# Quantised activations held as float16 multiples of 2^-24 instead of integers with an offset

## The reference

```python
u = (mu @ W_dec + b_dec).reshape(B, 257, 30)      # mu = cond: 2 x 128
param = einsum('bik,kj->bij', u, V)               # rank 30, V: 30 x 256
y = x @ param[:, :-1] + param[:, -1]              # x: 2 x 1024 x 256
quant_act(a)    = round(a * 127/max|a|_row) / (127/max|a|_row)
quant_weight(w) = clip(round(w / s), -1, 1) * s   # s = mean|w|
h = gelu(quant_act(y) @ quant_weight(w1).T)       # w1: 1024 x 256
out = x + quant_act(h) @ quant_weight(w2).T       # w2: 256 x 1024
```

## Time and profile before

| | us |
|---|---|
| median of 3 runs | 70.28 |
| lowest, highest | 69.92, 72.28 |
| profiled execution, its time | 69.81 |
| profiled execution, its span from the first to the last instruction | 68.0 |
| PE busy | 57.9 |
| DVE busy | 45.2 |
| ACT busy | 36.1 |
| POOL busy | 28.7 |

### The profile page before, as it was taken

One profiled execution on the slowest core, in us unless ns is written; L12 is line 12 of the kernel. 1 busy time (PEld: TensorE's weight loads), 2 busy tenths in 40 slices (PEclk: granted clock), 3 DMA queues, 4 the chain that ended last, 5 costly groups with the idle time before them and its releaser, 6 DMA issues.

```text
span 68.0 us, 1313 instructions
## 1 busy us (share of the span) xinstructions
PE 57.9 (85%) x463; PEld 31.8 (47%) x469; DVE 45.2 (66%) x92; ACT 36.1 (53%) x53; POOL 28.7 (42%) x46
## 2 busy tenths in 40 slices
PE   2977599998796799979999969999999999979910
PEld 0324132222432364433564823855859577869800
DVE  2000708475428784899999898499796979996520
ACT  3506005700067297999987826747959293753000
POOL 6500000000000109996848894674675828970000
PEclk9999999999999999999999999999999999999999
DMA  0899999999999999400199969699698999923052
GB/s 0 183 379 422 409 414 415 419 383 396 412 412 424 438 400 448 198 19 0 26 195 46 225 126 193 123 183 194 126 258 36 230 260 212 360 89 154 22 200 96
DMA packets 18343, 16.20 MB, mean 238 GB/s; under 512 B 14752, under 2 KB 15136, under 8 KB 17952
## 3 DMA queue, kind: packets, MB, share of 16 engines
q1 hardware_dynamic: 18192, 15.86, 77.8%
q10 hardware_dynamic: 144, 0.24, 2.0%
HBM read 10.47 MB, written 2.10 MB: 185 GB/s over the span
## 4 chain that ended last, share of the span: by engine, by line
PE 38%; DMA 20%; DVE 15%; SPq 9%; ACT 8%; issue 4%; POOL 2%; DVEq 0%
DMA w_dec_all<-in_w_dec_dram 17%; PE ps_h L471 13%; PE ps_o L492 8%; PE ps_z L492 6%; SPq L254 5%; ACT w_dec_all L617 4%; DMA yq_t<-yq_h 4%; DVE pair_max L726 3%; DVE h_max L744 3%; PE ps_y L443 3%; DVE o_sb L768 3%; SPq L271 2%; PE ps_z L431 2%; POOL hq_h L371 2%; ACT y_q L606 1%
## 5 line engine op out<-in xcount | busy, mean ns | idle before, releaser
L371 POOL TENSOR_SCALAR hq_h<-w_dec_all,pair_rcp 128x1024 f16<-128x1024 f32 x14 | 15.7, 1118 | 7.9 <-DVE pair_rcp L740 7.2
L471 PE MATMUL ps_h<-w_t,yq_t 128*128 128x512 bf16 x60 | 15.1, 380 | 1.4 <-DMA yq_t<-yq_h 0.7
L726 DVE TENSOR_REDUCE pair_max<-w_dec_all 128x2 f32<-128x2048 f32 x7 | 15.9, 2277 | 0.0
L617 ACT ACTIVATE w_dec_all<-ps_h,pair_c 128x1024 f32<-128x1024 f32 x10 | 10.9, 1113 | 6.6 <-PE ps_h L471 6.6
L397 PE MATMUL ps_h<-warm_h 128*128 128x512 bf16 x37 | 11.5, 424 | 1.5 <-POOL warm_h L313 1.3
L471 PEld LDWEIGHTS ps_h<-w_t,yq_t 128*128 128x128 bf16 x64 | 5.6, 98 | 8.4 <-issue 1.3
L329 POOL TENSOR_TENSOR c<-y_inv,s 128x2 f32<-128x2 f32 x3 | 0.6, 193 | 20.5 <-DVE y_inv L714 20.5
L492 PE MATMUL ps_o<-w_t,hq_t 128*128 128x256 f16 x64 | 8.3, 273 | 0.4 <-DVE o_sb L768 0.4
L492 PE MATMUL ps_z<-w_t,hq_t 128*128 128x256 f16 x64 | 8.3, 273 | 0.0
L589 ACT ACTIVATE w_abs<-w_sb 128x1024 f32<-128x1024 f32 (+1 forms) x3 | 2.7, 914 | 9.4 <-DMA w_sb<-in_w_tr_dram 9.3
L617 ACT ACTIVATE w_dec_all<-ps_h,c 128x1024 f32<-128x1024 f32 x6 | 6.8, 1133 | 0.5 <-PE ps_h L471 0.5
(11 more groups left out here) (90 smaller groups left out, 70.9 us busy)
## 6 DMA issues: line engine op xcount, KB each, us to landing
w_sb<-in_w_tr_dram SPq DMA_DIRECT2D x4, 512.0 KB, 9.0
x_sb<-in_x_dram SPq DMA_DIRECT2D x2, 1024.0 KB, 18.8
out_dram<-o_sb SPq DMA_DIRECT2D x7, 256.0 KB, 2.7
w_dec_all<-in_w_dec_dram SPq DMA_DIRECT2D x3, 512.0 KB, 7.9
w_dec_all<-in_w_dec_dram SPq DMA_DIRECT2D x3, 448.0 KB, 8.5
x_t<-in_x_tr_dram SPq DMA_DIRECT2D x1, 1024.0 KB, 16.5
w_dec_all<-in_w_dec_dram SPq DMA_DIRECT2D x1, 576.0 KB, 10.6
x_t<-in_x_tr_dram SPq DMA_DIRECT2D x2, 256.0 KB, 11.1
```

The lines of the kernel that those rows point to most:

```text
L371: pool.tensor_scalar(hq_h[n % NB][:, :], h_tile(n), scale, H_OFFSET, ALU.mult, ALU.add).then_inc(hq_ready, 1)
L471: last = nc.tensor.matmul(ps_h[k][:, half, :], yq_t[:, p, n % 2, c, :], w1_t[:, c, half * HALF:(half + 1) * HALF], start=(c == 0), stop=(c ...
L617: nc.scalar.activation(h_tile(n), ps_h[n % 2][:, :, :].rearrange("p a n -> p (a n)"), ACT.Gelu, scale=c1_of(n)).then_inc(gelu_done, 1)
L726: nc.vector.tensor_reduce(pair_max[:, p, 2:4], h_pair[p % NH], AXX, ALU.max, apply_absolute_value=True).then_inc(pair_max_ready, 1)
```

## The change

Rows are scaled by 127 * 2^-24 / max instead of 127 / max. The results are at most 127 multiples of 2^-24, the spacing of the smallest float16 numbers, so that a write to float16 rounds them to whole multiples with no offset. y_q becomes float16 and is transposed as it is, by PE or by the DMA; the copies out of PSUM move bit patterns as int16 and subtract nothing; w1's ternary values become float16. `narrow_y`, `offset_sums`, the copy on ACT, and the matmul with `offsets` in `product_2` go. The waits follow: SP's transpose_yq waits for ACT's quantise_y, and quantise_y(6) and (7) wait until the DMA has read the buffer of pairs 4 and 5. The 2^-24 is taken back by the factors per row, which are computed from the same scaled maxima. The diff, cut to its core:

```diff
-OFFSET = 16384.0
-MAGIC = 1.5 * 2 ** 23 + OFFSET
-H_OFFSET = 1024.0 + 128.0
+UNIT = 2.0 ** -24
...
-ident_h = sb("ident_h", [P, P], BF16)
-offsets = sb("offsets", [P, P], FP16)
-w1_t = sb("w1_t", [P, DC, H], BF16)
+w1_t = sb("w1_t", [P, DC, H], FP16)
-w2_off = sb("w2_off", [P, D], FP16)
...
-y_q = [sb(f"y_q{k}", [P, 2, D]) for k in range(2)]
-yq_h = [sb(f"yq_h{k}", [P, 2, D], BF16) for k in range(2)]
-yq_t = sb("yq_t", [P, NP, 2, DC, P], BF16)
+y_q = [sb(f"y_q{k}", [P, 2, D], FP16) for k in range(2)]
+yq_t = sb("yq_t", [P, NP, 2, DC, P], FP16)
...
-def low_half(t):
-    return t.bitcast(BF16).rearrange("p (n two) -> p n two", two=2)[:, :, 0]
-def blocks(bank, n, dt=BF16):
-    return bank[:, 0:n * P // 2].bitcast(dt).rearrange("p (c q) -> p c q", c=n)
-yq_low = [low_half(y_q[k][:, :, :].rearrange("p t c -> p (t c)")) for k in range(2)]
+def blocks(bank, n):
+    return bank[:, 0:n * P // 2].bitcast(FP16).rearrange("p (c q) -> p c q", c=n)
+yq_flat = [y_q[k][:, :, :].rearrange("p t c -> p (t c)") for k in range(2)]
-ps_off = ps_o[:, 0:D]
...
     def transpose_yq(p):
-        sp.wait_ge(yqh_ready, p - 3)
-        sp.dma_start_transpose(yq_t[:, p, :, :, :].rearrange("p t c q -> p (t c) q"),
-                               yq_h[p % 2][:, :, :].rearrange("p t c -> p (t c)")).then_inc(yqt_landed[p % 2], 16)
+        sp.wait_ge(yq_ready, 2 * p + 2)
+        sp.dma_start_transpose(yq_t[:, p, :, :, :].rearrange("p t c q -> p (t c) q"), yq_flat[p % 2]).then_inc(yqt_landed[p % 2], 16)
     def transpose_hq(n):
...
-    def narrow_y(p):
-        pool.wait_ge(yq_ready, 2 * p + 2)
-        if p >= 6:
-            pool.wait_ge(yqt_landed[p % 2], yqt_count(p - 2))
-        pool.tensor_scalar(yq_h[p % 2][:, :, :].rearrange("p t c -> p (t c)"),
-                           y_q[p % 2][:, :, :].rearrange("p t c -> p (t c)"), 1.0, -MAGIC,
-                           ALU.mult, ALU.add).then_inc(yqh_ready, 1)
     def part_of(w, n):
...
-        pool.tensor_scalar(hq_h[n % NB][:, :], h_tile(n), scale, H_OFFSET, ALU.mult, ALU.add).then_inc(hq_ready, 1)
+        pool.tensor_scalar(hq_h[n % NB][:, :], h_tile(n), scale, None, ALU.mult).then_inc(hq_ready, 1)
...
-        if 1 <= p < LATE_Y - AHEAD:
-            narrow_y(p + AHEAD)
-    pool.tensor_scalar(hq_h[(NT - 1) % NB][:, HALF:], h_tile(NT - 1)[:, HALF:], h_rcp[:, NT - 1:NT], H_OFFSET,
-                       ALU.mult, ALU.add).then_inc(last_hq[1], 1)
+    pool.tensor_scalar(hq_h[(NT - 1) % NB][:, HALF:], h_tile(NT - 1)[:, HALF:], h_rcp[:, NT - 1:NT], None,
+                       ALU.mult).then_inc(last_hq[1], 1)
...
     def total(k, part):
-    def offset_sums():
-        pe.wait_ge(yqt_copied, EARLY_YQT)
-        for n in range(2):
-            pe.wait_ge(s_w2q[n], 1)
-        pe.wait_ge(s_identf, 1)
-        for t in range(HC):
-            last = nc.tensor.matmul(ps_off, ident_f[:, :], w2_t[:, t, :], start=(t == 0), stop=(t == HC - 1))
-        last.then_inc(s_offsum, 1)
     def product_z(q, halves=range(DC)):
...
-            last = nc.tensor.transpose(ps_yqt[n][:, c - DC * i0, :], yq_low[p % 2][:, c * P:(c + 1) * P], ident_h[:, :])
+            last = nc.tensor.transpose(ps_yqt[n][:, c - DC * i0, :], yq_flat[p % 2][:, c * P:(c + 1) * P], ident_f[:, :])
     def product_1(n):
...
     def product_2(n):
-            pe.wait_ge(s_offs, 1)
-            pe.wait_ge(s_w2off, 1)
+            pe.wait_ge(yqt_copied, EARLY_YQT)
+            for part in range(2):
+                pe.wait_ge(s_w2q[part], 1)
-            nc.tensor.matmul(o_of[n], offsets[:, :], w2_off[:, :], start=True, stop=False)
-            last = nc.tensor.matmul(o_of[n], hq_t[k][:, t, :], w2_t[:, t, :], start=(n >= LATE and t == 0), stop=(t == HC - 1))
+            last = nc.tensor.matmul(o_of[n], hq_t[k][:, t, :], w2_t[:, t, :], start=(t == 0), stop=(t == HC - 1))
     def transpose_hq(n, half):
...
     def quantise_y(p):
-            act.wait_ge(yqh_ready, p - 5)
+            act.wait_ge(yqt_landed[p % 2], yqt_count(p - 2))
...
-                                 bias=MAGIC, scale=scale).then_inc(yq_ready, 1)
+                                 scale=scale).then_inc(yq_ready, 1)
     def gelu(n):
...
     def copy_yqt(n):
-        nc.scalar.activation(yq_t[:, p, :, :, :].rearrange("p t c q -> p (t c) q"), ps_yqt[n].bitcast(I16), ACT.Copy,
-                             bias=-OFFSET).then_inc(yqt_copied, 1)
+        nc.scalar.activation(yq_t[:, p, :, :, :].rearrange("p t c q -> p (t c) q").bitcast(I16),
+                             ps_yqt[n].bitcast(I16), ACT.Copy).then_inc(yqt_copied, 1)
...
-        if p == AHEAD + 2:
-            act.wait_ge(s_offsum, 1)
-            nc.scalar.activation(w2_off[:, :], ps_off, ACT.Copy, scale=-1.0).then_inc(s_w2off, 1)
...
-        nc.scalar.activation(hq_t[n % LAG][:, part, :], ps_hqt[n][half], ACT.Copy,
-                             bias=-H_OFFSET).then_inc(late_copied[n][half], 1)
+        nc.scalar.activation(hq_t[n % LAG][:, part, :].bitcast(I16), ps_hqt[n][half].bitcast(I16),
+                             ACT.Copy).then_inc(late_copied[n][half], 1)
 def _(dve):
-    def copy_q(dst, src):
-        return nc.vector.tensor_scalar(dst, src.bitcast(I16), -OFFSET, None, ALU.add)
     def magnitudes(w_part, part, done):
...
     def y_scales(p, i0=0, i1=2):
-        nc.vector.tensor_scalar(y_inv[:, p, i0:i1], y_max[p][:, i0:i1], EPS, 1.0 / QMAX,
+        nc.vector.tensor_scalar(y_inv[:, p, i0:i1], y_max[p][:, i0:i1], EPS, 1.0 / (QMAX * UNIT),
...
     def copy_yqt(n):
-        copy_q(yq_t[:, p, i0:i1, :, :].rearrange("p t c q -> p (t c) q"), ps_yqt[n]).then_inc(yqt_copied, 1)
+        nc.vector.tensor_copy(yq_t[:, p, i0:i1, :, :].rearrange("p t c q -> p (t c) q").bitcast(I16),
+                              ps_yqt[n].bitcast(I16)).then_inc(yqt_copied, 1)
     def pair_h_maximum(p):
...
-        nc.vector.tensor_scalar(hq_t[n % LAG][:, part, :], ps_hqt[n][half], -H_OFFSET, None,
-                                ALU.add).then_inc(late_copied[n][half], 1)
+        nc.vector.tensor_copy(hq_t[n % LAG][:, part, :].bitcast(I16),
+                              ps_hqt[n][half].bitcast(I16)).then_inc(late_copied[n][half], 1)
...
-    nc.vector.tensor_scalar(hq_h[(NT - 1) % NB][:, 0:HALF], h_tile(NT - 1)[:, 0:HALF], h_rcp[:, NT - 1:NT], H_OFFSET,
-                            ALU.mult, ALU.add).then_inc(last_hq[0], 1)
+    nc.vector.tensor_scalar(hq_h[(NT - 1) % NB][:, 0:HALF], h_tile(NT - 1)[:, 0:HALF], h_rcp[:, NT - 1:NT], None,
+                            ALU.mult).then_inc(last_hq[0], 1)
```

More of the change, by code:

```diff
@@ L163, in adaln_ffn @@
         late_bank = {LATE: ps_y, LATE + 1: ps_h[0], LATE + 2: ps_y, LATE + 3: ps_h[1]}
-        ps_hqt = {n: [blocks(late_bank[n][:, half, :], HC // 2, FP16) for half in range(2)] for n in late_bank}
+        ps_hqt = {n: [blocks(late_bank[n][:, half, :], HC // 2) for half in range(2)] for n in late_bank}
         o_of = [(ps_o, ps_z)[n % 2][:, 0:D] for n in range(NT)]
@@ L179, in adaln_ffn @@
         s_ident = sem("ident_ready")
-        s_identh = sem("ident_bf16_ready")
         s_identf = sem("ident_fp16_ready")
-        s_offs = sem("offsets_ready")
         s_ones = sem("ones_ready")
@@ L199, in adaln_ffn @@
         s_wall = sem("weight_total_ready")
-        s_offsum = sem("w2_row_sums")
-        s_w2off = sem("w2_offsets_ready")
         z_done = sem("z_done")
@@ L210, in adaln_ffn @@
         yq_ready = sem("yq_ready")
-        yqh_ready = sem("yq_bf16_ready")
         yqt_done = sem("first_quad_yq_transposed")
@@ L320, in _ @@
             pool.wait_ge(s_ident, 1)
-            pool.tensor_copy(ident_h[:, :], ident[:, :]).then_inc(s_identh, 1)
             pool.tensor_copy(ident_f[:, :], ident[:, :]).then_inc(s_identf, 1)
-            pool.memset(offsets[:, :], H_OFFSET).then_inc(s_offs, 1)
             def scale_y(p):
@@ L538, in _ @@
             keep_warm(4)
-            pe.wait_ge(s_identh, 1)
+            pe.wait_ge(s_identf, 1)
             transpose_yq(0)
@@ L569, in _ @@
                 product_1(2 * p)
-                if p == LAG // 2:
-                    offset_sums()
                 if p + 2 < NP:
@@ L736, in pair_scales @@
                 dve.wait_ge(pair_max_ready, 2 * p + 2 if p < Y_PAIRS else p + 1 + Y_PAIRS)
-                nc.vector.tensor_scalar(pair_inv[:, p, cols], pair_max[:, p, cols], EPS, 1.0 / QMAX,
+                nc.vector.tensor_scalar(pair_inv[:, p, cols], pair_max[:, p, cols], EPS, 1.0 / (QMAX * UNIT),
                                         ALU.max, ALU.mult).then_inc(pair_inv_ready, 1)
@@ L748, in h_scales @@
                 dve.wait_ge(h_max_ready, n - SINGLE + 1)
-                nc.vector.tensor_scalar(h_inv[:, n:n + 1], h_max[:, n:n + 1], EPS, 1.0 / QMAX,
+                nc.vector.tensor_scalar(h_inv[:, n:n + 1], h_max[:, n:n + 1], EPS, 1.0 / (QMAX * UNIT),
                                         ALU.max, ALU.mult).then_inc(h_inv_ready, 1)
```

## The result

The changed kernel took 84.63 us (median of 4 runs, 84.42 to 84.78) against 70.1 for the kernel before (now of 4 runs, where the 70.28 was of 3): a ratio of 1.2085, 95% interval 1.2015 to 1.2155. That is the first rival, forecast at 85.8 us with a chance of 0.42. The forecast of 69.3 us was wrong.

What follows compares the result with a forecast made beforehand. PE was taken to set the pace from 40.2 to 55.9 us, after waits on POOL and SP's queue and before DVE; seven offset products save 0.77 us, all else zero, giving 69.3 us (own range 68.7 to 70.2, with rival 1 68.6 to 87.0).

Steps and rivals of the forecast that it cites:

- rival 1: POOL becomes the bound: one-operation quantise costs L352's 2.85 us a tile, pairs take 6.2 us; 85.8 us, chance 0.42.
- The one unknown: POOL's quantise: POOL's quantise, multiplication alone on fourteen and a half tiles: taken at 1118 ns, bounds -0.3 and +1.73 us a tile.
- the tail: After POOL's half tile: four transposes 0.5, copy 0.6, half a product_2 0.45, output 0.5, then 2.6 us to the span's end.
- The sum for the other case: POOL's quantise staying at 1118 ns: seven offset products on the path save 0.77 us, for 69.3 us.
- the stage: PE sets the pace between 40.2 and 55.9 us, product_1(8) to output(8); seven offset products of 0.11 there save 0.77 us.
- The row sums: offset_sums on PE, 1.04 us: only 0.14 us comes free, in front of PE's idle time; nothing gained.
- the narrowing: narrow_y on POOL, three instructions of 0.62 us: SP's queue covers them, so removing them gains nothing.
- the added waits: quantise_y(6) and (7) on ACT wait for transfers of pairs 4 and 5; over 3 us to spare, price zero.
- the copies: Copies out of PSUM on ACT and DVE keep sizes and counts: zero, bounds -0.1 and +0.2 us for a DVE copy.
- Rival 2: SP's queue takes the gain: late yq transfers of pairs 5 and 6 cost 0.2 to 0.5 us; 69.6 to 69.9, chance 0.12.

Runs made afterwards that it cites:

- e1_add_zero: Changed kernel with POOL's quantise written as a multiplication and an addition of 0.0, likewise for the last half tile; 69.68 us, ratio 0.987 to the kernel before.
- e3_before_swap: Kernel before with POOL's w2 rounding to int16 given an addition of 0.0 and its narrowing of yq made an addition alone; 69.97 us.
- e8_no_offset: Kernel before without the offset products, row sums and ACT copy, h keeping its 1152; 69.26 us, ratio 0.987.
- e9_add_zero_again: Changed kernel with the addition of 0.0 in POOL's quantise, measured once more in a second series; 69.84 us, ratio 0.994 to the kernel before.
- e7_narrow_back: Changed kernel with 0.0 added in POOL's quantise and POOL's copy of yq put back ahead of SP's transposes; 69.85 us, ratio 1.000 to the kernel before.
- e11_narrow_again: Second-series run of the changed kernel with 0.0 added in POOL's quantise and POOL's copy of yq put back; 69.46 us, ratio 0.989.

## Why the prediction was wrong

**The unknown that decided.** The step that failed is "The one unknown: POOL's quantise". It had both ends right, 1118 and 2846 ns, and took the lower one, though its own chances gave rival 1 more (0.42) than the forecast (0.40). Its reasons were that the changed instruction differs from L371 in one operation and from L352 in the type written, and that the cast shows no penalty for having less to do. The first reason counts differences, though nothing in the trace said which difference costs. The second compares with another opcode. What the runs showed in its place is 2842 ns for the multiplication alone, because the second operation is absent: with it, float16 takes 1120 ns (e1_add_zero) and int16 1119 (e3_before_swap). The row of the same form (L352) was the better neighbour than the row of the same place.

Of the two rules quoted there, that of the Trainium skill's "GPSIMD: programming the Q7 cores", Data Types and Layout (with conversion on, every element goes through the same converter on the write port, whatever its type), says nothing of time; the use that the prediction made of it agrees with the runs, where int16 took 1119 ns and float16 1118 to 1120. The one of the Trainium skill's "GPSIMD Engine Reference", Elementwise — side-by-side cycle accounting, on bodies of up to two operations doesn't hold for this instruction: its single operation took 2842 ns, 2.78 ns an element, and its two took 1118.

**The price of rival 1** was 1.2 us too high against the median (85.8 against 84.63). That it came so close is in part luck, since two terms were off and partly cancelled. Most pairs take 5.81 us and not 6.16, since the small gaps of rows 5 are gone where POOL doesn't wait; with a start 0.3 us earlier (31.05 for 31.36) the half tile ends at 76.9 (75.32 + 1.56) instead of 79.2. Against that the tail is 6.0 us and not 4.8 (its listed terms add up to 4.65): PE's order keeps product_2(12) behind the transposes of tile 14, so four products follow POOL's last whole tile and not a half.

**The sum for the other case** held in its main term: the stage lost 0.73 us where 0.77 was forecast, e8_no_offset came out 0.9 us faster, and the repaired kernel's median was 69.68 and 69.84, where 69.3 (own range 68.7 to 70.2) was said for POOL at 1118 ns. It did not hold in what it took as fixed. The stage's start moved from 40.21 to 40.67 in e1_add_zero and to 41.08 in e9_add_zero_again, and the last output starts at 64.72 and 65.31, where it started at 64.94 before. So the profiled executions (69.67 and 70.06 us, against 69.81) don't show the 0.77 arriving at the end; only the ratios over several executions point that way.

**The row sums, the narrowing, the added waits and the copies** were taken at zero. The narrowing is tested (e7_narrow_back, e11_narrow_again), and the row sums go with the offset products in e8_no_offset, whose interval ends at 1.5 us and has no room for 0.77 and another 0.87. The copies of 128x512 on ACT took 595 ns and those on DVE 425, about as before. The waits that were added held nothing up in e1_add_zero: ACT's quantising of y waited for DVE's scales alone, 0.2 us in total over the ten tiles of this group, and SP issued each transfer of yq within 0.05 us of the end of the issue in front of it.

**Rival 2, SP's queue.** It stood in the wrong place. PE didn't wait for yq of pairs 5 and 6, but the wait for pair 4 grew from 0.66 us to 1.60 in e1_add_zero and 2.12 in e9_add_zero_again. Of the first 0.94 us, 0.46 is a later start; the rest is PE coming to the wait earlier, as matmuls in front of it are gone. The transfer took 3.5 and 4.0 us to land where it had taken 2.5. In e9_add_zero_again SP's queue was held up in the transposes of h behind it, in e1_add_zero already while issuing it, 2.26 us instead of 1.28:

```profile
37.09 2.26 SPq L249 DMA_TRANSPOSE yq_t<-y_q  x1
```

The moved bytes of the stretch from 32 to 41 us, in 40 slices of 0.225 us, show what was going on (e1_add_zero, then e8_no_offset, then the kernel before):

```profile
GB/s 0 0 0 0 0 0 32 212 215 209 208 179 131 200 200 213 215 203 114 0 0 73 121 205 196 55 0 1 8 10 9 165 291 268 249 168 4 0 65 218
```

```profile
GB/s 0 0 0 0 0 0 0 2 170 218 212 204 196 152 89 215 210 208 212 187 53 5 73 56 203 200 114 5 0 1 8 9 9 157 291 269 261 165 1 0
```

```profile
GB/s 0 0 0 0 0 0 0 16 197 221 206 206 189 123 203 213 181 53 2 1 8 10 9 168 290 269 258 206 215 195 168 200 216 122 7 0 59 213 216 216
```

For about 1.1 us, from 37.9 in the first and from 38.3 in the second, almost nothing moves, and both times it is the transfer of yq of pair 4 that is under way. The kernel before has such a pause too, from 36.1 us, but there transposes of h are under way, and it is over before the transfer of yq starts at 37.64. With the copy put back it comes at 34.7 (e7_narrow_back) and again misses yq, which lands in 2.5 us. So the pause isn't new with the change; where it falls differs from kernel to kernel, and where it fell on the transfer that PE waits for, product_1(8) started 0.46 (e1_add_zero) and 0.87 us (e9_add_zero_again) later than before. What it is, and what places it, wasn't tried and stays open.

## What to carry to other kernels

An operation taken out of an instruction isn't free until a row of the new form says so. Before dropping an offset on POOL, write it as 0.0 and keep the pair times-plus: that one edit was worth 15 us here. The second operation must be one whose pair is known to be fast: plus 0.0 took 1120 ns, minus 0.0 took 3700. And when two neighbours bound an unknown price, ask for each feature in which they differ whether another row of the same engine separates it; where none does, the chance is even and the price is a reason to measure.

## What the runs showed of the hardware

POOL's tensor_scalar over 128x1024, float32 in: 1118 to 1124 ns for times-plus, times-times and plus-times; 2770 for times a constant alone, 2842 to 2862 for times a scalar per row alone; 3700 for times-minimum, times-maximum and times-minus; 1119 with int16 out for times-plus. An addition alone over 128x512 took 1498, times-plus of the same size 617. On DVE a multiplication alone over 128x512 took 488 ns and one with an addition 486. Multiples of 2^-24 in float16 cost nothing extra where the repaired kernel (e1_add_zero) uses them: PE's product_1 stayed at 380 ns a matmul, ACT's quantising of y at 477, POOL's of h at 1120. The profiles of the kernel before and of all repaired kernels have, between 34 and 41 us and amid DMA transposes, a pause of about 1.1 us in which some 10 GB/s or less move.
